# Flamingo block with a routed expert layer: the scores of a batch computed jointly, and the attention loop reordered on every engine

## The chip, the cores and the metric

The kernel runs on one core of a Trainium2 chip. The metric is the device time of one execution in microseconds (us), lower is better. A core has five engines with a queue of their own each: TensorE (PE in the profile; PEld are its weight loads), VectorE (DVE), ScalarE (ACT), GpSimd (POOL) and SyncE (SP), which issues DMAs. They run their queues in order and wait for one another through semaphores.

## The reference

```python
x = x + tanh(g_xattn) * xattn(layernorm(x), ctx)          # x: 16 x 128 x 128, ctx: 16 x 77 x 96
x = x + tanh(g_ffn) * experts(layernorm(x))

def xattn(x, y):                                          # 16 heads of 8
    q = x @ Wq.T + bq;  k, v = split(y @ Wkv.T + bkv)
    att = softmax(q @ k.T / sqrt(8))                      # per head, 128 x 77
    return (att @ v) @ Wo.T + bo

def experts(x):                                           # 4 rounds, 4 experts, top 2
    for r in range(4):
        w = softmax over the 2 largest of x @ Wg[r] + bg[r]
        x = x + sum_e w[e] * (gelu(x @ W1[e] + b1[e]) @ W2[e] + b2[e])
    return x
```

All is float32. Matmuls that need it are split in a high and a low part (float32r) and done as three passes: high by high, high by low, low by high.

## The kernel before

The 16 batches form four chunks of four. A prologue loads and transposes the weights and makes K, Q and V of chunk 0. Then comes the attention loop, one step per batch b = 0 to 15, and then the expert part, 64 units (round, chunk, expert) of 24 matmuls each, whose code the change leaves alone.

Step b of the loop works on several batches at once. TensorE computes the scores of batch b+1 (`scores`, line 1217), transposes the probabilities of batch b in three groups (`transpose_probs`, 1234; keys ("PT", b, 0..2)), multiplies those of batch b-1 with the values and, for the sums, with ones (`weigh_values`, 1246), and projects the output of batch b-2 (`project_o`, 1268). Scores of a batch lie in four PSUM banks, one per group of four heads (q = 0 to 3); each uses 32 rows of the array. They are made in two halves, q = 0, 1 and q = 2, 3: half 0 early in the step, half 1 after the products with the values. Half 0 is read by VectorE (`smallest`, 864: the minimum per head; `shift`, 874: subtracts it into `shifted`) and ScalarE takes one exponential of 616 columns from there. Half 1 is read by VectorE for the minimum and by ScalarE in eight exponentials of 77 columns straight from PSUM (`exponentials`, 665). The halves of the next batch may be written when those are done.

The rest of the probabilities' way: ScalarE copies each transposed group to SBUF (`move_pt`, 681), VectorE divides the product by the sums (`normalise_o`, 884: reciprocal and product) and adds the residual (`add_residual`, 893). In between, steps carry the work of the next chunk: by r = b % 4 the context is transposed and K made (r = 0), x transposed and Q made (r = 1), VectorE's low part of Q (`low_q`, 843; r = 2), V made (r = 3). Tables name the step for others: NORMALISE for VectorE's normalising of x of chunks 2 and 3, MOMENTS for the means and variances, SPLIT_X, ROUTER and WEIGHTS slots for the routing of the first two chunks. At b = 3 VectorE also splits the router weights (lines 1100 to 1111).

GpSimd multiplies K of batch b+2 with a head mask (`stage_k`, 551: a masked copy, a masked rounded copy, and their difference), adds the bias to x (`add_bias`, 567), and splits an eighth of the expert weights in each step of W_AT, one step later (W_LAG). It needs the weights that its own casting DMAs brought (lines 587 and 589).

Transposes and projections share two PSUM banks in turn (`next_job`): a job may be written when the last but one has been read. The order of all of it is written out by hand in one loop per engine; TensorE's is

```python
if b + 1 < B: scores(b + 1, 0)
transpose_probs(b, 0)
...
if b >= 1: weigh_values(b - 1)
if b + 1 < B: scores(b + 1, 1)
transpose_probs(b, 1)
transpose_probs(b, 2)
if b >= 2: project_o(b - 2)
```

with the chunk work between, and an extra pair of matmuls on the identity before group 2 (WARM_PT) whose result is not used. ScalarE's order is copy of group 0, long exponential of b+1, copies of groups 1 and 2, eight short exponentials of b+1.

## Time and profile before

| | us |
|---|---|
| median of the timed executions | 489.18 |
| all three | 489.18, 484.53, 489.44 |
| the profiled execution | 485.13 |
| its span, first to last instruction | 483.4 |
| granted TensorE clock, mean | 0.996 of full |

Rows of the profile give a start in us from the beginning of the span, a duration, the engine, the line of the kernel, the operation with output and inputs, and how many instructions are merged (xN). Durations overlap slightly where an engine is pipelined, so what one instruction costs is best read from start to start. What stands in brackets is how long the engine had been idle and who ended it.

### The profile page before, as it was taken

How to read it: one execution, taken by the hardware profiler on the slowest of the kernel's cores; microseconds unless marked ns; L12 is line 12 of the kernel's file. 1: busy time of each engine (PE TensorE's matmuls, PEld its weight loads, DVE VectorE, ACT ScalarE, POOL GpSimd, SP SyncE). 2: the span in 40 equal slices, each digit the busy share in tenths (PEclk: the TensorE clock that was granted, in tenths of full speed). 3: DMA queues.
4: the chain of work that ended last, by engine and by line, in shares of the span. 5: the costliest groups of instructions: out<-in, count | busy, mean ns of one | idle time of the engine just before them, and what ended most of it. 6: DMA issues, size and time to landing. Idle time of an engine off the chain costs nothing.

```text
span 483.4 us, 9118 instructions
## 1 busy us (share of the span) xinstructions
PE 471.8 (98%) x3007; PEld 383.4 (79%) x3007; DVE 374.6 (77%) x750; ACT 383.0 (79%) x783; POOL 82.8 (17%) x133
## 2 busy tenths in 40 slices
PE   7799999989999999999999999999999999999997
PEld 6578787878888788888888888888888888888885
DVE  4869888897888867876887687778777976886776
ACT  2588888769787887988788788869886988798773
POOL 6567597920500000000000000000000000000000
PEclk9899999999999999999999999999999999999999
DMA  5920000004002020030031004000400040014001
GB/s 146 296 75 15 3 15 3 14 1 177 2 0 89 1 89 0 22 155 1 1 120 57 1 0 177 0 1 1 176 0 0 4 174 1 1 43 155 23 1 44
DMA packets 15173, 25.21 MB, mean 52 GB/s; under 512 B 3505, under 2 KB 11542, under 8 KB 13078
## 3 DMA queue, kind: packets, MB, share of 16 engines
q1 hardware_dynamic: 11152, 22.05, 13.3%
q0 software_dynamic: 2592, 2.10, 2.1%
q10 hardware_dynamic: 1382, 0.49, 0.5%
q8 instruction: 24, 0.39, 0.3%
q14 instruction: 23, 0.19, 0.1%
HBM read 22.82 MB, written 1.18 MB: 50 GB/s over the span
## 4 chain that ended last, share of the span: by engine, by line
PE 92%; DVE 4%; issue 2%; ACT 1%; POOL 1%; ACTq 0%; POOLq 0%; DVEq 0%
PE ps L1361 12%; PE ps L1348 12%; PE ps L1363 12%; PE ps L1362 12%; PE ps L1350 12%; PE ps L1349 12%; PE ps L1243 5%; PE ps L1230 3%; PE ps L1259 3%; PE ps L1169 2%; PE ps L1264 2%; PE ps L1271 1%; DVE xn L840 1%; PE ps L1204 1%; PE ps L1314 1%
## 5 line engine op out<-in xcount | busy, mean ns | idle before, releaser
L922 DVE TENSOR_TENSOR h_lo<-g_sb,h_hi 128x512 fp32r<-128x512 f32 x256 | 169.9, 687 | 75.5 <-ACT h_hi L786 75.4
L779 ACT ACTIVATE g_sb<-ps,cols 128x512 f32<-128x512 f32 x256 | 174.7, 693 | 35.2 <-PE ps L1350 34.2
L786 ACT ACTIVATE h_hi<-g_sb 128x512 fp32r<-128x512 f32 x256 | 155.8, 640 | 0.0
L1361 PE MATMUL ps<-h_hi,w_hi 128*128 128x512 f32 x252 | 101.5, 403 | 0.0
L1348 PE MATMUL ps<-x_hi,w_hi 128*128 128x512 f32 x256 | 101.1, 395 | 0.0
L1350 PE MATMUL ps<-x_hi,w_lo 128*128 128x512 f32 x256 | 100.1, 391 | 0.0
L1349 PE MATMUL ps<-x_lo,w_hi 128*128 128x512 f32 x256 | 99.8, 390 | 0.0
L1363 PE MATMUL ps<-h_hi,w_lo 128*128 128x512 f32 x252 | 99.6, 395 | 0.0
L1362 PE MATMUL ps<-h_lo,w_hi 128*128 128x512 f32 x252 | 99.5, 395 | 0.0
L1350 PEld LDWEIGHTS ps<-x_hi,w_lo 128*128 128x128 f32 x256 | 48.0, 188 | 11.3
L1349 PEld LDWEIGHTS ps<-x_lo,w_hi 128*128 128x128 f32 x256 | 48.1, 188 | 10.9
L1348 PEld LDWEIGHTS ps<-x_hi,w_hi 128*128 128x128 f32 x256 | 48.0, 188 | 10.9 <-issue 0.2
L1363 PEld LDWEIGHTS ps<-h_hi,w_lo 128*128 128x128 f32 x252 | 47.2, 187 | 11.8
L1361 PEld LDWEIGHTS ps<-h_hi,w_hi 128*128 128x128 f32 x252 | 47.3, 188 | 11.0
L1362 PEld LDWEIGHTS ps<-h_lo,w_hi 128*128 128x128 f32 x252 | 47.3, 188 | 10.3
L943 DVE TENSOR_TENSOR cur<-cur,contrib 128x512 f32<-128x512 f32 x63 | 43.1, 684 | 0.0
L686 ACT ACTIVATE probT<-ps 103x512 f32<-103x512 f32 x48 | 29.3, 613 | 11.1 <-PE ps L1243 10.1
L871 DVE TENSOR_REDUCE least<-ps 128x8 f32<-128x616 f32 x32 | 25.4, 793 | 11.2 <-PE ps L1230 11.1
L1243 PE MATMUL ps<-ident,prob 128*103 128x128 f32 (+1 forms) x192 | 31.4, 286 | 0.0
L677 ACT ACTIVATE prob<-ps,least 128x77 f32<-128x77 f32 x128 | 29.2, 345 | 1.1 <-DVE least L871 1.1
L1243 PEld LDWEIGHTS ps<-ident,prob 128*103 128x103 f32 (+1 forms) x192 | 22.5, 162 | 5.7 <-issue 4.5
L932 DVE SCALAR_TENSOR_TENSOR contrib<-ps,cols,cwb_even 128x512 f32<-128x512 f32 x32 | 23.9, 746 | 1.1 <-PE ps L1363 1.0
(149 smaller groups left out, 492.6 us busy)
## 6 DMA issues: line engine op xcount, KB each, us to landing
cwb_even<-cw_rows SPq DMA_DIRECT2D x8, 1024.0 KB, 5.3
cwb_odd<-cw_rows SPq DMA_DIRECT2D x8, 1024.0 KB, 4.7
w_hi<-in_L_ffn_W_dram POOLq DMA_DIRECT2D x2, 1024.0 KB, 13.4
x_sb<-in_x_dram SPq DMA_DIRECT2D x4, 256.0 KB, 7.6
w_in<-in_L_ffn_W_dram SPq DMA_DIRECT2D x1, 1024.0 KB, 5.7
out_dram<-xn SPq DMA_DIRECT2D x3, 256.0 KB, 2.3
ctx_sb<-in_ctx_dram ACTq DMA_DIRECT2D x4, 115.5 KB
v_st<-v_sb SPq DMA_DIRECT2D x8, 38.5 KB
```

The lines of the kernel that those rows point to most:

```text
L686: nc.scalar.activation(probT[0:RP, b % 2, PG * g:PG * (g + 1), :], bank(("PT", b, g))[0:RP, :].rearrange("p (c l) -> p c l", l=L), ACT.Cop ...
L779: nc.scalar.activation(g_sb[:, k, :], ps[:, k, :], ACT.Gelu_apprx_tanh, bias=b1_c[:, e * NF + k:e * NF + k + 1]).then_inc(gelu_done, 1)
L786: nc.scalar.activation(h_hi[:, u % 2, k, :], g_sb[:, k, :], ACT.Copy).then_inc(hi_done, 1)
L922: nc.vector.tensor_tensor(h_lo[:, u % 2, k, :], g_sb[:, k, :], h_hi[:, u % 2, k, :].bitcast(F32), ALU.subtract).then_inc(lo_done, 1)
L943: nc.vector.tensor_tensor(cc, cc, contrib[:, u % 2, :], ALU.add).then_inc(added, 1)
L1243: t = tr(bank(key)[0:n, k * L:(k + 1) * L], prob[:, b % 2, at:at + n], ident[:, :])
L1348: mm(ps[:, k, :], w1_hi[:, w], x_hi[:, c, :], start=True, stop=False)
L1349: mm(ps[:, k, :], w1_hi[:, w], x_lo[:, c, :], start=False, stop=False)
L1350: mm(ps[:, k, :], w1_lo[:, w], x_hi[:, c, :], start=False, stop=True).then_inc(w1_done, 1)
L1361: mm(yb, w2_hi[:, w], hh, start=k == 0, stop=False)
L1362: mm(yb, w2_hi[:, w], hl, start=False, stop=False)
L1363: m = mm(yb, w2_lo[:, w], hh, start=False, stop=k == NF - 1)
```

## The change

The scores of a batch are made in one set: each of the three passes runs over all four groups q, and the set waits for the subtraction and for all short exponentials of the batch before. All loops are reordered: TensorE does scores, groups 2 and 1, projection of b-2, chunk work, group 0, values of b-1; ScalarE copies groups 2 and 1, does the short exponentials, copies group 0, does the long one; VectorE starts a step with the division and the minimum of half 1. VectorE, not ScalarE, copies group 2 of step 0 and group 0 of step 11 (PT_DVE). K is split in high and low once per chunk (`split_k`, for chunk 0 `split_k0` on VectorE), so that staging it takes two masked copies and no difference. The bias is added to four batches in one instruction. The warm pair in the loop is gone; some of the prologue's are moved, and the prologue is reordered. The two casting DMAs of the expert weights are issued by GpSimd in steps 1 and 0 of the loop. MOMENTS, NORMALISE, SPLIT_X, W_AT and other slots shift by a step in places; low_q runs in r = 1. In both kernels x of chunks 2 and 3 is normalised on VectorE (NORMALISE_P, the table for GpSimd, is empty).

```diff
-        XT_AT = (10, 12)
+        XT_AT = (10, 14)
-        GATE0_SLOT = 13
+        GATE0_SLOT = 14
-        WEIGHTS0_SLOT = 15
+        WEIGHTS0_SLOT = 14
-        WARM_PT = (0, 0, 1)
-        R_LOW = 2
+        R_LOW = 1
+        R_LK = 2
+        PT_DVE = {0: 2, 11: 0}
+        FIRST_E = 1
+        WD_AT = (1, 0)
...
-        NORMALISE = {4: 2, 8: 3}
-        MOMENTS = {1: (0, 2), 5: (0, 3), 7: (1, 0), 10: (1, 1), 14: (1, 2)}
-        SPLIT_X = {11: 0, 13: 1}
+        NORMALISE = {3: 2, 8: 3}
+        NORMALISE_P = {}
+        MOMENTS = {0: (0, 2), 3: (0, 3), 7: (1, 0), 10: (1, 1), 15: (1, 2)}
+        SPLIT_X = {11: 0, 14: 1}
...
-        W_AT = (2, 3, 5, 6, 8, 10, 11, 13)
+        W_AT = (3, 4, 6, 7, 8, 9, 10, 13)
...
+            def split_k(c):
+
+                at = slice(TC * M * c, TC * M * (c + 1))
+                moved(pool, ("K", c))
+                pool.wait_ge(k_split, 2 * c)
+                nc.gpsimd.tensor_copy(kT_r[:, :], kT[:, at]).then_inc(k_split, 1)
+                pool.wait_ge(k_split, 2 * c + 1)
+                nc.gpsimd.tensor_tensor(kT_lo[:, at], kT[:, at], kT_r[:, :].bitcast(F32),
+                                        ALU.subtract).then_inc(k_split, 1)
...
-                nc.gpsimd.tensor_tensor(k_f[:, :, :], kb, headm, ALU.mult).then_inc(k_stage, 1)
-                nc.gpsimd.tensor_tensor(k_hi[:, s, :].rearrange("p (h m) -> p h m", m=M), kb, headm,
+                nc.gpsimd.tensor_tensor(k_hi[:, s, :].rearrange("p (h m) -> p h m", m=M),
+                                        kT[:, at].unsqueeze(1).to_broadcast([P, HQ, M]), headm,
                                         ALU.mult).then_inc(k_stage, 1)
-                pool.wait_ge(k_stage, 3 * b + 2)
-                nc.gpsimd.tensor_tensor(k_lo[:, s, :], k_f[:, :, :].rearrange("p h m -> p (h m)"), k_hi[:, s, :].bitcast(F32),
-                                        ALU.subtract).then_inc(k_stage, 1)
+                nc.gpsimd.tensor_tensor(k_lo[:, s, :].rearrange("p (h m) -> p h m", m=M),
+                                        kT_lo[:, at].unsqueeze(1).to_broadcast([P, HQ, M]), headm,
+                                        ALU.mult).then_inc(k_stage, 1)
...
-            def scores(b, half):
+            def scores(b):
 
                 c, at = b // TC, slice(b % TC * L, b % TC * L + L)
-                if half == 0:
-                    moved(pe, ("Q", part_of(b)))
-                    pe.wait_ge(k_stage, 3 * b + 3)
-                if b >= 1 and half == 0:
+                moved(pe, ("Q", part_of(b)))
+                pe.wait_ge(k_stage, 2 * b + 2)
+                if b >= 1:
                     pe.wait_ge(sub_done, b)
-                if b >= 1 and half == 1:
-                    pe.wait_ge(exp_done, 2 * b)
+                    pe.wait_ge(exp_done[1], b)
                 for n, (qs, ks) in enumerate(passes):
-                    for q in (2 * half, 2 * half + 1):
+                    for q in range(NQ):
```

TensorE, in a step with r = 3 of before, from the first half of the scores to the second; L1230 are scores, L1243 transposes of probabilities, L1259 and L1264 the products with values and ones.

```order
L1230 MATMUL ps<-k_hi,q_hi 128x308 x2
L1230 MATMUL ps<-k_lo,q_hi 128x308 x2
L1230 MATMUL ps<-k_hi,q_lo 128x308 x2
L1243 MATMUL ps<-ident,prob 103x128 x2
L1243 MATMUL ps<-ident,prob 102x128
L1243 MATMUL ps<-ident,prob 103x128
L1259 MATMUL ps<-probT,v_st 32x128 x12
L1264 MATMUL ps<-probT,row_head 32x128 x12
L1230 MATMUL ps<-k_hi,q_hi 128x308 x2
L1230 MATMUL ps<-k_lo,q_hi 128x308 x2
L1230 MATMUL ps<-k_hi,q_lo 128x308 x2
```

The same engine and kind of step in the kernel after; L1285 are scores, L1300 the transposes, L1330 the projection (the products with the values follow later, after group 0).

```order
L1285 MATMUL ps<-k_hi,q_hi 128x308 x4
L1285 MATMUL ps<-k_lo,q_hi 128x308 x4
L1285 MATMUL ps<-k_hi,q_lo 128x308 x4
L1300 MATMUL ps<-ident,prob 102x128
L1300 MATMUL ps<-ident,prob 103x128 x2
L1300 MATMUL ps<-ident,prob 102x128
L1300 MATMUL ps<-ident,prob 103x128
L1300 MATMUL ps<-ident,prob 102x128
L1300 MATMUL ps<-ident,prob 103x128 x2
L1330 MATMUL ps<-wT,oT_sb 128x128
```

The six pairs of scores have become three groups of four at the head of the step, and the products with the values have moved from its middle to its end.

VectorE in step 3 of before, from the minimum of half 1 to the start of step 4's normalising; L1102 to L1110 are the split of the router weights, L897 the residual, L871 the minima, L880 the subtraction, L887 and L891 the division, L840 the normalising of chunk 2.

```order
L871 TENSOR_REDUCE least<-ps 128x8
L1102 CAST wg_s<-wg_in 128x4x4
L1104 TENSOR_TENSOR wg_s<-wg_in,wg_s 128x4x4
L1108 CAST wg_w<-wg_in 128x16x4
L1110 TENSOR_TENSOR wg_w<-wg_in,wg_w 128x16x4
L897 SCALAR_TENSOR_TENSOR x_sb<-ps,tgates,x_sb 128x128
L871 TENSOR_REDUCE least<-ps 128x8
L880 TENSOR_TENSOR shifted<-ps,least 128x616
L887 RECIPROCAL rT_sb<-ps 128x128
L891 TENSOR_TENSOR oT_sb<-ps,rT_sb 128x128
L840 TENSOR_SCALAR xn<-x_sb,mv,rstd 128x128 x4
```

VectorE in step 3 of after, from the minimum of half 1 to the end of the step; L1141 to L1149 are the split, L882 the normalising of chunk 2, L873 and L876 the moments of chunk 3.

```order
L917 TENSOR_REDUCE least<-ps 128x8
L951 SCALAR_TENSOR_TENSOR x_sb<-ps,tgates,x_sb 128x128
L1141 CAST wg_s<-wg_in 128x4x4
L1143 TENSOR_TENSOR wg_s<-wg_in,wg_s 128x4x4
L1147 CAST wg_w<-wg_in 128x16x4
L1149 TENSOR_TENSOR wg_w<-wg_in,wg_w 128x16x4
L917 TENSOR_REDUCE least<-ps 128x8
L926 TENSOR_TENSOR shifted<-ps,least 128x616
L882 TENSOR_SCALAR xn<-x_sb,mv,rstd 128x128 x4
L873 BN_STATS stats<-x_sb 128x6 x4
L876 BN_AGGR mv<-stats 128x2 x4
```

The split now stands ahead of the second minimum and the subtraction, and the normalising and the moments have moved into the same step.

ScalarE in step 0 of before: L686 copies, L671 long and L677 short exponentials, L626 context, L643 K.

```order
L686 ACTIVATE probT<-ps 103x512
L626 ACTIVATE ctxT<-ps 96x308
L671 ACTIVATE prob<-shifted 128x616
L686 ACTIVATE probT<-ps 103x512 x2
L643 ACTIVATE kT<-ps,cols 128x308
L677 ACTIVATE prob<-ps,least 128x77 x8
```

ScalarE in step 0 of after, with the end of the prologue ahead of it: L693 x and L701 Q of batches 1 to 3, L716 short and L710 long exponentials, L785 the wide bias, L665 context, L725 copies, L682 K.

```order
L716 ACTIVATE prob<-ps,least 128x77 x8
L693 ACTIVATE xnT<-ps 128x384
L701 ACTIVATE q_hi<-ps,bq_s 128x384
L710 ACTIVATE prob<-shifted 128x616
L785 ACTIVATE bv_w<-ident,cols 128x128
L665 ACTIVATE ctxT<-ps 96x308
L725 ACTIVATE probT<-ps 103x512
L716 ACTIVATE prob<-ps,least 128x77 x8
L682 ACTIVATE kT<-ps,cols 128x308
L725 ACTIVATE probT<-ps 103x512
L710 ACTIVATE prob<-shifted 128x616
```

The short exponentials of batch 0 stand ahead of x and Q of batches 1 to 3, and in the loop the short ones come before the long one.

## Rows read from the trace of the kernel before

**Rows 1.** Stretches of the core: each engine's busy us, clock, DMA share, GB/s.

```profile
19.52:108.77 89.25, 87.36 (x1239) 71.21 (x1238) 74.59 (x172) 72.48 (x209) 64.14 (x97) 0.99 0.11 33
200.00:300.00 100.00, 100.00 (x437) 80.90 (x436) 77.39 (x143) 82.88 (x154) 0.00 (x0) 1.00 0.14 57
```

The columns of rows 1 are the stretch, its length, then PE, PEld, DVE, ACT and POOL busy with their instructions, the granted clock of PE, the DMA share and GB/s.

**Rows 2.** Timeline of PE, step 6 to 7: start us, us, engine, line.

```profile
55.96 0.41 PE L1230 MATMUL ps<-k_hi,q_hi 32*128 32x308 f32 x2
...
56.57 0.68 PE L1243 MATMUL ps<-ident,prob 128*103 128x128 f32 x4
57.09 0.39 PE L1169 MATMUL ps<-ident 128*128 128x128 f32 x2
57.31 0.60 PE L1243 MATMUL ps<-ident,prob 128*102 128x128 f32 x4
...
59.30 0.89 PE L1259 MATMUL ps<-probT,v_st 103*32 103x128 f32 x24
...
60.78 0.41 PE L1230 MATMUL ps<-k_hi,q_hi 32*128 32x308 f32 x2
```

**Rows 3.** Timeline of PE, the first scores of the kernel.

```profile
13.20 0.43 PE L1230 MATMUL ps<-k_hi,q_hi 32*128 32x308 f32 x4
...
13.58 0.34 PE L1230 MATMUL ps<-k_hi,q_lo 32*128 32x308 f32 x4
```

**Rows 4.** Timeline of ACT, steps 0 and 1.

```profile
25.09 1.83 ACT L677 ACTIVATE prob<-ps,least 128x77 f32<-128x77 f32 x8
26.75 0.66 ACT L686 ACTIVATE probT<-ps 103x512 f32<-103x512 f32 x1
27.23 0.67 ACT L654 ACTIVATE xnT<-ps 128x512 f32<-128x512 f32 x1
27.71 0.80 ACT L671 ACTIVATE prob<-shifted 128x616 f32<-128x616 f32 x1
```

**Rows 5.** Groups of DVE, 26.92 to 106.5: count, busy us, mean ns, idle before.

```profile
L871 DVE TENSOR_REDUCE least<-ps 128x8 f32<-128x616 f32 x27 | 21.4, 794 | 9.2 <-PE ps L1230 9.1
L887 DVE RECIPROCAL rT_sb<-ps 128x128 f32<-128x128 f32 x14 | 13.3, 947 | 0.0
L880 DVE TENSOR_TENSOR shifted<-ps,least 128x616 f32<-128x616 f32 x14 | 11.2, 798 | 0.4
L897 DVE SCALAR_TENSOR_TENSOR x_sb<-ps,tgates,x_sb 128x128 f32<-128x128 f32 x13 | 4.4, 336 | 1.7 <-PE ps L1271 1.4
...
L891 DVE TENSOR_TENSOR oT_sb<-ps,rT_sb 128x128 f32<-128x128 f32 x14 | 4.1, 292 | 0.5
```

**Rows 6.** Timeline of DVE, chunk work at five places.

```profile
13.06 2.31 DVE L840 TENSOR_SCALAR xn<-x_sb,mv,rstd 128x128 f32<-128x128 f32 x3
...
39.78 0.16 DVE L1102 CAST wg_s<-wg_in 128x16 fp32r<-128x16 f32 x1
...
40.69 0.82 DVE L1110 TENSOR_TENSOR wg_w<-wg_in,wg_w 128x64 fp32r<-128x64 f32 x1
...
44.82 1.90 DVE L840 TENSOR_SCALAR xn<-x_sb,mv,rstd 128x128 f32<-128x128 f32 x4
...
67.26 1.16 DVE L840 TENSOR_SCALAR xn<-x_sb,mv,rstd 128x128 f32<-128x128 f32 x4
...
103.86 0.86 DVE L831 BATCH_NORM_STATS2 stats<-x_sb 128x6 f32<-128x128 f32 x4
```

**Rows 7.** Timeline, three marks: second scores, last exponentials, first expert matmul.

```profile
19.52 0.62 PE L1230 MATMUL ps<-k_hi,q_hi 32*128 32x308 f32 x2
...
104.67 1.83 ACT L677 ACTIVATE prob<-ps,least 128x77 f32<-128x77 f32 x8
...
108.77 0.47 PE L1348 MATMUL ps<-x_hi,w_hi 128*128 128x512 f32 x1
```

**Rows 8.** DMA issues: count, KB each, median us from issue to landing.

```profile
w_hi<-in_L_ffn_W_dram POOLq DMA_DIRECT2D x2, 1024.0 KB, 13.4
```

**Rows 9.** Groups of POOL, 26.92 to 106.5: the masked copies of K.

```profile
L561 POOL TENSOR_TENSOR k_hi<-kT,head_mask 128x308 fp32r<-128x308 f32 x12 | 8.5, 706 | 0.0
```

More of the change, by code:

```diff
@@ L368, in bank, with probs_read @@
             return ps[:, jobs[key][2], :]
+        def probs_read(b):
+            return max(jobs[("PT", b, g)][0] for g in range(3)) + 1
         LN = [(0, "a"), (0, "b"), (0, 1), (0, 2), (0, 3), (1, 0), (1, 1), (1, 2), (1, 3)]
@@ L665, in exponentials @@
             def exponentials(b, half):
[L667 to L668 removed]
+                if b >= 2 and half == FIRST_E:
+                    act.wait_ge(job_mm, probs_read(b - 2))
                 if half == 0:
@@ L1111, in _ @@
                                             ALU.subtract).then_inc(wg_split, 1)
+                if b + 1 < B:
+                    smallest(b + 1, 0)
+                if b == WEIGHTS0_SLOT:
+                    weights(0)
+                if b + 1 < B:
+                    shift(b + 1)
+                if b == ROUTER0_SLOT:
+                    router(0)
+                if b in SPLIT_X:
+                    split_x(SPLIT_X[b])
+                if b in NORMALISE:
+                    normalise(NORMALISE[b])
+                if b in MOMENTS:
+                    moments(*MOMENTS[b])
+                if b == ROUTER1_SLOT:
+                    router(1)
+                if c < NC and r == R_LOW:
+                    low_q(c)
             normalise_o(B - 2)
+            weights(1)
             add_residual(B - 3)
-            weights(1)
             normalise_o(B - 1)
@@ L1248, in weigh_values @@
                 c = b // TC
-                moved(pe, ("PT", b, 2))
+                pe.wait_ge(job_act, max(read_no[("PT", b, g)] for g in range(3) if PT_DVE.get(b) != g))
+                if b in PT_DVE:
+                    moved(pe, ("PT", b, PT_DVE[b]))
                 pe.wait_ge(v_ld[c], 16 * len(pieces))
```

314 lines of the change are left out of this document (164 added, 150 removed).

## The prediction, made before the changed kernel was run

> **What bounds the kernel now.** I read the busy table in stretches first, because the kernel has two halves with different limits. From 200 to 300 us (the mixture of experts) TensorE is busy 100.00 of 100 us and VectorE and ScalarE 77.39 and 82.88 [rows 1]; that code is the same in both kernels, so it can only start earlier or later. The attention loop, 19.52 to 108.77 us, shows TensorE 87.36, VectorE 74.59, ScalarE 72.48, GpSimd 64.14 of 89.25 us [rows 1]. Over its 16 steps (b = 0 to 15, the last one partly) TensorE is the bound, but by little: divided by 15 steps, VectorE has 4.97 us of work per step and ScalarE 4.83 us, against 5.95 us that pass. So no more than about 1 us a step can be won, whatever TensorE is relieved of.
>
> Second, the order of time on TensorE in one step without chunk work, 55.96 to 60.78 us [rows 2]: half of the scores 0.61 (55.96 to 56.57), a transpose group 0.52, two warm instructions 0.22, and so on without a hole, the other half of the scores among it, the two products with the values 1.48 (59.30 to 60.78): 4.82 us, all TensorE.
>
> Third, the first scores of the kernel, the only place where both halves stand back to back with nothing between them [rows 3]: the twelve matmuls (three groups of four) start at 13.20 and the last ends at 13.58 + 0.34 = 13.92, 0.72 us. Half of them alone takes 0.61 to the next instruction. Four row groups of the array thus run side by side, and a joint set costs what half a set costs.
>
> **The change, part by part.** TensorE: each step loses one half of scores, 0.61, and the warm pair, 0.22, from rows 2: 0.83 us. A plain step falls from 4.82 to 3.99, one with chunk work by as much. Over 14 steps that is 11.6 us of TensorE, if TensorE still set the pace. It does not.
>
> ScalarE after: per step the eight short exponentials 1.83 busy (25.09), a copy every 0.48 when they stand in a row (26.75, 27.23, 27.71), the long exponential 0.80 [rows 4]: 1.8 + 3 x 0.48 + 0.8 = 4.0 us, and some 0.8 of chunk work on average (4.83 in all, above). The order changes: eight short ones first, the long one last.
>
> VectorE after: two minima at 0.79, the subtraction 0.80, reciprocal 0.95, product 0.29, residual 0.34 [rows 5]: 3.96 us, 3.8 with the overlap of neighbours. The joint scores couple them more tightly: the scores of batch b+1 need the subtraction of b AND all exponentials of the short half of b, and both minima now wait for one signal. In a plain step: scores 0.7, minimum 0.8, residual 0.3, minimum 0.8, subtraction 0.8 gives 3.4 us from one set of scores to the next, below ScalarE's 4.0 to 4.5; this chain alone costs nothing. What costs is chunk work in front of it. Two probability copies move to VectorE (steps 0 and 11, 0.65 us each by the nearest row, 0.79 for a 616-wide read, at most; at least 0.48, ScalarE's).
>
> Step 3 is the crowded one. VectorE now has the split of the router weights (39.78 to 40.69 + 0.82, so 1.73), the normalising of chunk 2 (1.90 for four in step 4 of before) and the moments of chunk 3 (0.86 for the four statistics and 0.4 behind them) [rows 6] in one step; before they stood in steps 3, 4 and 5. With its 3.8 of its own this makes 8.3 us, and a product that TensorE waits for (the output projection) stands behind it.
>
> I laid the three queues side by side with these prices, those of the chunk work from rows 6 and the like, the orders of before and after, and the waits of the code. From the end of the last exponential of step 0 to that of step 14, the steps 1 to 14 come out as 5.2, 4.55, 5.3, 6.9, 5.45, 4.55, 4.45, 5.25, 5.8, 4.55, 5.85, 4.95, 4.0, 5.95: 72.75 us. Steps near 4.5 are ScalarE's plus a wait for the first minimum; 5.2 to 5.8 are those where K and the context, or x and Q of the next chunk, pass through ScalarE and TensorE in turn; 6.9 is step 4, which pays step 3's backlog; 5.85 and 5.95 are VectorE's (split of x, router and weights). Before, the same stretch runs from 25.09 + 1.83 = 26.92 [rows 4] to 104.67 + 1.83 = 106.50 [rows 7], 79.58 us. Won: 6.8 us.
>
> Prologue: K is split on VectorE before it is staged, so the first scores come 0.6 late; the eight short exponentials of batch 0 (1.83) now stand before x of batches 1 to 3 is moved for Q; and the bias product waits behind the long one. The second scores start at some 22.3 instead of 19.52 [rows 7]. As all exponentials of batch 0 are done by then, step 0 is shorter, and its end moves only from 26.92 to 27.95: lost 1.0 us.
>
> Tail: before, the first matmul of the experts comes 108.77 - 106.50 = 2.27 us after the last exponential [rows 7]. After, more stands between them: the transposes that need the long exponential, the weights' transpose, the output projection, which waits 1 us for VectorE (behind the split of x), router logits 1.1, a transpose group 0.55 and the value products 1.48 [rows 2]: 5.2 us. Lost: 2.9 us.
>
> Sum: -6.8 + 1.0 + 2.9 = -2.9; I add 0.05 us per step for hand-overs that the layout took at nothing (14 x 0.05): -2.2 us. GpSimd loses one of three products per batch and gains two short splits per chunk, and stays a step ahead; its cast loads of the expert weights move from the start into steps 0 and 1. They took 13.4 us from issue to landing [rows 8]; issued at about 27 and 30 they are there by 44, and the first split of weights in step 4 stands near 43: a wait of about 1 us, covered, since the K that GpSimd stages behind it is wanted near 48.7.
>
> The profiled execution took 485.13 us with a span of 483.4, so the sum gives 482.9. The three timed executions of before are 489.18, 484.53 and 489.44: two levels 4.5 us apart, whatever the kernel does. Against the median the same sum gives 487.0. I name the middle, 485.0 us, and let the range hold both.
>
> **Rivals.** Packed: the backlog of step 3 is absorbed and steps fall to the 4.97 us that VectorE needs (14 x 4.97 = 69.6): another 3.1 us less, 479.8 against the profile, 483.8 against the median. For it: VectorE's idle time before the minima in the loop, 9.2 us [rows 5], was a wait for scores that now come at once. Against it: VectorE's chunk work is lumped, and the loop that joins the scores leaves no half to work on meanwhile. To reach it the gain must be 5.3 us, just over 1% (4.9 us, about what a measurement of this kernel can tell from no change).
>
> VectorE slowed by GpSimd: three normalisings took 2.31 beside GpSimd's products (13.06), 0.77 each, against 1.90 and 1.16 for four at 44.82 and 67.26 [rows 6]; and a subtraction of 64 elements per partition took 0.82 where a cast of 16 took 0.16 [rows 6]. If both normalisings of the loop meet GpSimd like that, each costs 4 x 0.77 = 3.1 instead of the 1.5 that I took (between the two), and as VectorE sets steps 4 and 9 both times show: +3.2, so 1.0 us slower than before, 486.1 against the profile, 490.2 against the median. It decides from 2.6 us each on. For it: GpSimd is busy 72% of the loop [rows 1]. Against it: one product of 0.71 less on GpSimd per batch [rows 9]. The Trainium skill (SBUF — State Buffer, Who interferes with whom) states that a tensor_scalar in a two-port mode and a GpSimd instruction exclude each other for a whole instruction, the later one blocking fully. By that rule, as an estimate, each of four would wait for a GpSimd product, 4 x (0.29 + 0.71) = 4.0 [rows 6, 9], two times 2.5 more than I took, and the sum would be 2.8 us slower than before; the row of 2.31 fits it, the row of 1.90 shows half of it.
>
> Weights late: the cast loads, issued in the loop, are squeezed behind the plain loads of the same weights and the values' small transfers and land after 45.8, from when K of batch 6 is late. At twice 13.4 us behind the second issue, 57, the loss is 11 us: slower by 9, 494. Against it: the transfers of that stretch are few (the x, context and projection loads are over by then), so landing should be quicker, not slower.
>
> **How the numbers follow.** Forecast (within 1%) 0.55, packed 0.2, slowed VectorE 0.17, weights late 0.08. Faster by over 1%: the packed case and a little of the forecast's own spread, 0.28. Slower by over 1%: late weights and the bad end of the slowed case, 0.11. Within 1%: 0.61. The range runs from 479.5 (packed, lower level) to 489.6 (slowed, upper level).
>
> **What would show it.** Right: joint scores as three groups of four in 0.72 us or less; loop steps of 4.5 without and 5.2 to 5.8 with chunk work, the step after the router-weight split near 7; TensorE with real holes in the loop, waiting for exponentials and minima; second scores near 22, last exponential near 101.4, first expert matmul 106 to 107; the expert half unchanged at some 375 us (483.4 - 108.77). Wrong: if joint scores take 1.2 us, the array did not run four groups; if step 4 is 5.3, the packed case holds; if GpSimd waits at its first weight split for more than 3 us, the loads were late; if the expert half differs by over 1 us, the clock or the router's tail has moved.

## The result and the profile after

| | before | after |
|---|---|---|
| median, us | 485.08 (484.42 to 489.44, 20 executions) | 488.62 (485.45 to 491.81, 20 executions) |
| ratio after / before | | 1.0055, interval 1.0033 to 1.0077 |
| profiled execution, us | 485.13 | 485.45 |
| its span, granted clock | 483.4, 0.996 | 483.7, 0.993 |

The change makes the kernel 0.55% slower; the forecast was a small gain (482.9 against the profile, 485.0 named). By the ratio that is 2.7 us (the medians lie 3.5 apart). Between the two profiled executions the difference is only 0.3 us; the rest is not in these two traces at all, and that is the lesson of this case. In what follows a hole is a stretch in which TensorE stands idle between two matmuls; half clock is the lower level of its granted clock; warm pairs are matmuls on the identity whose result is not used.

The busy table in stretches, kernel after. The columns are those of [rows 1]: stretch, length, then PE, PEld, DVE, ACT, POOL busy, PE's clock, DMA share, GB/s.

```profile
26.00:27.00 1.00, 0.92 (x2) 0.75 (x3) 0.96 (x3) 1.00 (x7) 0.96 (x3) 0.52 0.44 119
27.00:31.00 4.00, 4.00 (x25) 3.13 (x24) 3.24 (x12) 2.56 (x6) 3.83 (x6) 0.50 2.02 291
...
32.00:34.00 2.00, 2.00 (x8) 1.10 (x6) 0.00 (x0) 1.74 (x7) 0.00 (x0) 0.78 0.97 275
34.00:104.70 70.70, 65.30 (x1079) 52.06 (x1078) 62.72 (x135) 60.30 (x176) 44.04 (x61) 1.00 0.04 10
...
200.00:300.00 100.00, 100.00 (x437) 81.00 (x436) 77.45 (x144) 82.77 (x155) 0.00 (x0) 1.00 0.15 59
```

The expert half is what it was. In the loop TensorE is no longer the bound: busy 65.30 of 70.70 us, VectorE 62.72, ScalarE 60.30. The column to look at is PE's clock. From about 26 to 32.8 us it is half of full (0.50 is the lower of the two levels, 1.2 GHz against 2.4). In the trace of before there is such a stretch too, of half the length and earlier:

```profile
17.20:20.60 3.40, 3.40 (x17) 2.57 (x15) 3.09 (x13) 2.73 (x11) 1.88 (x3) 0.50 2.05 253
21.00:25.00 4.00, 3.58 (x31) 2.64 (x29) 2.23 (x4) 3.09 (x7) 3.81 (x7) 1.00 1.02 370
```

What TensorE did before the clock fell, kernel after: its timeline in step 0.

```profile
21.86 0.31 PE L1285 MATMUL ps<-k_hi,q_lo 32*128 32x308 f32 x4
22.11 0.47 PE L1235 MATMUL ps<-ident,ctx_sb 77*96 77x77 f32 x4
22.42 1.36 PE L1300 MATMUL ps<-ident,prob 128*102 128x128 f32 x8
26.08 1.39 PE L1243 MATMUL ps<-ctxT,wT 96*128 96x308 f32 x2 [2.30 <-DVE probT L935]
27.27 1.06 PE L1300 MATMUL ps<-ident,prob 128*103 128x128 f32 x4
```

It stands still from 23.78 to 26.08, and the next matmuls take 1.39 and 1.06 us, where at full clock the same two groups take 0.79 and 0.68 (in the run with the normalising moved, below). The releaser in brackets is VectorE's copy of a transposed group. VectorE at the same time:

```profile
21.86 2.86 DVE L882 TENSOR_SCALAR xn<-x_sb,mv,rstd 128x128 f32<-128x128 f32 x4
24.64 0.79 DVE L917 TENSOR_REDUCE least<-ps 128x8 f32<-128x616 f32 x1
25.35 0.67 DVE L935 COPY probT<-ps 103x512 f32<-103x512 f32 x1
```

and GpSimd beside it:

```profile
22.03 1.29 POOL L603 TENSOR_TENSOR x_sb<-x_sb,bo_row 128x512 f32<-128x512 f32 x1 [1.01 <-DVE bo_row L1125]
23.29 0.69 POOL L591 TENSOR_TENSOR k_hi<-kT,head_mask 128x308 fp32r<-128x308 f32 x1
23.95 0.69 POOL L594 TENSOR_TENSOR k_lo<-kT_lo,head_mask 128x308 fp32r<-128x308 f32 x1
```

Four normalisings of chunk 1 take 2.86 us, where the best four of before took 1.16 [rows 6]. They stand ahead of a minimum and a copy that everything waits for, and they meet GpSimd's products, the first of which is the new bias addition for four batches at once. Read one by one, the four take 0.34, 1.30, 0.73 and 0.74 us: the last three are about as long as the three products beside them (1.29, 0.69, 0.69), and each ends 0.08 or 0.09 us after one of them. In the kernel before, the same four stood ahead of `bo_row`, the bias row that GpSimd's addition waits for:

```profile
19.59 1.17 DVE L840 TENSOR_SCALAR xn<-x_sb,mv,rstd 128x128 f32<-128x128 f32 x4 [0.27 <-POOL rstd L539]
```

They were over at 20.76, and GpSimd's addition began at 21.11. In the kernel after they stand behind `bo_row`, which ends at 21.94 and so releases GpSimd's addition (22.03) just as they begin.

The rest of the profile after answers to the prediction's list. The first scores, and the wait of step 4:

```profile
14.08 0.41 PE L1285 MATMUL ps<-k_hi,q_hi 32*128 32x308 f32 x4 [0.97 <-DVE k_lo L907]
...
14.44 0.34 PE L1285 MATMUL ps<-k_hi,q_lo 32*128 32x308 f32 x4
...
46.27 0.41 PE L1285 MATMUL ps<-k_hi,q_hi 32*128 32x308 f32 x4 [1.33 <-DVE shifted L926]
```

A joint set takes 14.44 + 0.34 - 14.08 = 0.70 us, as [rows 3] said, and the first one starts 0.88 us later than in before. VectorE in step 3, the router split that stands ahead of the second minimum (L917) and of the subtraction that row 46.27 waits for:

```profile
41.88 0.49 DVE L1141 CAST wg_s<-wg_in 128x16 fp32r<-128x16 f32 x1
42.40 0.62 DVE L1143 TENSOR_TENSOR wg_s<-wg_in,wg_s 128x16 fp32r<-128x16 f32 x1
42.95 0.79 DVE L1147 CAST wg_w<-wg_in 128x64 fp32r<-128x64 f32 x1
43.77 0.70 DVE L1149 TENSOR_TENSOR wg_w<-wg_in,wg_w 128x64 fp32r<-128x64 f32 x1
44.39 0.79 DVE L917 TENSOR_REDUCE least<-ps 128x8 f32<-128x616 f32 x1
45.22 0.80 DVE L926 TENSOR_TENSOR shifted<-ps,least 128x616 f32<-128x616 f32 x1
45.93 1.11 DVE L882 TENSOR_SCALAR xn<-x_sb,mv,rstd 128x128 f32<-128x128 f32 x4
```

VectorE's groups in the loop (29.57 to 104.66), answering to [rows 5]:

```profile
L917 DVE TENSOR_REDUCE least<-ps 128x8 f32<-128x616 f32 x28 | 22.0, 790 | 0.7 <-PE ps L1285 0.7
L941 DVE RECIPROCAL rT_sb<-ps 128x128 f32<-128x128 f32 x14 | 13.3, 949 | 1.7 <-PE ps L1323 1.7
```

The idle time ahead of the minima has gone from 9.2 to 0.7 us: VectorE no longer waits for scores, scores wait for it. From the end of one step's last exponential to the next's, steps 1 to 14 take 6.69, 4.61, 5.90, 6.77, 5.44, 4.61, 4.26, 5.91, 5.56, 5.33, 4.71, 5.23, 4.27, 5.80: 75.09 us, from 29.57 to 104.66 (before 79.58). The tail: last exponential of step 14, then the first matmul of the experts.

```profile
103.87 0.79 ACT L710 ACTIVATE prob<-shifted 128x616 f32<-128x616 f32 x1
...
109.09 0.50 PE L1407 MATMUL ps<-x_hi,w_hi 128*128 128x512 f32 x1
```

And the weights' cast loads, in the DMA issues:

```profile
w_hi<-in_L_ffn_W_dram POOLq DMA_DIRECT2D x2, 1024.0 KB, 8.1
```

### The profile page after: what moved, and what is told of

It reads as the page before. It is cut to its first block, busy times and chain, and to the rows that moved or that the text cites. A ratio compares the mean times of both kernels' runs of the same rounds, so it can differ in the third digit from the quotient of the medians.

```text
span 483.7 us, 9099 instructions
## 1 busy us (share of the span) xinstructions
PE 464.2 (96%) x2989; PEld 375.8 (78%) x2989; DVE 376.2 (78%) x753; ACT 381.0 (79%) x781; POOL 72.3 (15%) x112
## 4 chain that ended last, share of the span: by engine, by line
PE 85%; DVE 7%; issue 3%; ACT 2%; DMA 1%; SPq 1%; DVEq 0%; ACTq 0%
PE ps L1420 12%; PE ps L1407 12%; PE ps L1422 12%; PE ps L1421 12%; PE ps L1409 12%; PE ps L1408 12%; PE ps L1300 3%; PE ps L1318 2%; PE ps L1323 2%; DMA gates<-in_g_ffn_dram 1%; PE ps L1285 1%; DVE least L917 1%; DVE rT_sb L941 1%; PE ps L1261 1%; DVE xn L882 1%
## 5 line engine op out<-in xcount | busy, mean ns | idle before, releaser
L725 ACT ACTIVATE probT<-ps 103x512 f32<-103x512 f32 x46 | 27.4, 616 | 9.4 <-PE ps L1300 9.2
L716 ACT ACTIVATE prob<-ps,least 128x77 f32<-128x77 f32 x128 | 29.3, 349 | 5.1 <-DVE least L917 5.0
L1300 PE MATMUL ps<-ident,prob 128*103 128x128 f32 (+1 forms) x192 | 30.5, 294 | 1.0 <-issue 0.4
L1300 PEld LDWEIGHTS ps<-ident,prob 128*103 128x103 f32 (+1 forms) x192 | 23.4, 169 | 7.0 <-ACT probT L725 2.8
L917 DVE TENSOR_REDUCE least<-ps 128x8 f32<-128x616 f32 x32 | 25.0, 789 | 0.7 <-PE ps L1285 0.7
L741 ACT ACTIVATE th<-half_d 128x32 f32<-128x32 f32 (+1 forms) x10 | 2.2, 225 | 28.7 <-DVE half_d L1046 28.7
```

Source lines behind the costliest of these rows:

```text
L917: nc.vector.tensor_reduce(least[:, b % 2, :].rearrange("p (q h) -> p q h", q=NQ)[:, two, :], scores, AX.X, ALU.min).then_inc(least_done[ha ...
L1300: t = tr(bank(key)[0:n, k * L:(k + 1) * L], prob[:, b % 2, at:at + n], ident[:, :])
```

## The granted clock separates the executions of one kernel

Every timed execution comes with its span and mean granted clock. Sorted by clock, before is a ladder: of 35 executions beside the first experiments 13 have 0.996 and 484.25 to 484.97 us, 4 have 0.993 and 485.8 to 486.1, 12 have 0.991 and 486.2 to 486.5, 6 have 0.985 or 0.986 and 489.1 to 489.4. After has one at 0.993 (485.45, the one that was profiled), four at 0.989 or 0.984 (486.5 to 487.8), ten at 0.985 or 0.986 (488.2 to 489.5), five at 0.981 or 0.978 (490.3 to 491.8). Time at half clock is 2 x (1 - clock) x span; the mean is 7.6 us for before and 15.0 us for after. A line through each kernel's executions costs 0.44 us (before) and 0.40 us (after) per us of half clock, and reaches full clock at 482.8 and 482.9. Put in the two means, the lines give 0.40 x 15.0 - 0.44 x 7.6 + 0.1 = 2.8 us, which is 488.93 - 486.15. That the two agree is no test, since a fitted line always goes through its means; what the lines say is that the kernels' times lie close to one common line and differ in where on it they are.

One limit holds for all comparisons with after below: after was timed in one series of 20 executions, and no run repeats it beside the variants. The ratios, each against before of the same series, are the safer measure.

So two theories went to the chip. A: the change made holes in TensorE's work, the one of 2.3 us in step 0 first, after which the clock is halved, and more so in most executions than in the profiled one. B: the pairs of warm matmuls that the change removed from the loop had kept the clock up.

## Experiments

All are edits of the kernel after unless it is said. Each ratio is against before on the same chip.

**1. The copy of step 0 back to ScalarE.**

```diff
-        PT_DVE = {0: 2, 11: 0}
+        PT_DVE = {11: 0}
```

> Edit: in the changed kernel the copy of probability group 2 of step 0 goes back from VectorE to ScalarE; nothing else. In the profile of the changed kernel TensorE stands idle for 2.3 us (23.8 to 26.1) until VectorE has made that copy, behind 2.86 us of normalising, and its granted clock falls to half at 26 for 6.8 us. Theory A (the median is slow because that hole lowers the clock): the hole shrinks to some 0.7 us, the last exponential of step 0 comes 1 us or more earlier, the mean granted clock of the executions rises from 0.986 towards 0.993, and the median falls by 2 to 4 us, to 485 to 487. Theory B (the clock is a bystander and the time lies in the lengthened prologue and tail): the median falls by the 1 us of step 0 at most, clock as it is.

Measured: 486.92 us (485.98 to 488.54), ratio 1.0022 (1.0000 to 1.0043), 10.3 us at half clock. The copy was not what mattered: the hole moved behind it, as long as before.

```profile
25.43 0.68 PE L1300 MATMUL ps<-ident,prob 128*103 128x128 f32 x4
28.40 0.46 PE L1285 MATMUL ps<-k_hi,q_hi 32*128 32x308 f32 x4 [2.29 <-POOL k_lo L594]
```

The bracket names GpSimd's k_lo, but K of this batch was staged by 25.6 (that of the next one ended at 28.37, by chance just before; in run 5 the same scores start ahead of it). What the scores wait for stands on VectorE and ScalarE of this run, in order of time:

```profile
22.82 2.87 DVE L882 TENSOR_SCALAR xn<-x_sb,mv,rstd 128x128 f32<-128x128 f32 x4
25.61 1.49 DVE L917 TENSOR_REDUCE least<-ps 128x8 f32<-128x616 f32 x2
...
26.43 1.83 ACT L716 ACTIVATE prob<-ps,least 128x77 f32<-128x77 f32 x8 [1.05 <-DVE least L917]
```

Normalising, minimum, short exponentials (to 28.26), scores at 28.40. The cause of the hole is the normalising, whoever copies. The last exponential of step 0 is not earlier (29.76), and yet there is less half clock than the 15.0 us of after. This run serves below as a control: it keeps a hole of 2.29 us.

**2. The hole of step 0 filled with ten warm pairs.**

```diff
                 transpose_probs(b, 1)
+                if b == 0:
+                    moved(pe, ("V", 0))
+                    warm(ps[:, 7, 0:P], 10)
```

> Edit: in the changed kernel ten warm matmuls on the identity (20 instructions, some 2.2 us at full clock) stand in that hole of step 0, written to a free bank; TensorE would wait there anyway, so no wait is taken away. Theory A: the granted clock stays up in the loop, step 1 falls from 6.7 to about 5.3 us, mean clock 0.99 or more, median 2 to 4 us lower. Theory B: no change of the median beyond 0.5 us, even where the clock is higher.

Measured: 485.99 (483.95 to 486.77), ratio 0.9985 (0.9960 to 1.0010), 5.0 us at half clock. No dependency is shorter, TensorE does more, and the kernel is 2.6 us faster than after; the intervals of the two ratios do not touch. Against run 1, which keeps the hole and was timed in the same series, the means are 485.65 and 487.24, and the half clock 5.0 against 10.3 us. Its trace:

```profile
23.55 2.40 PE L1226 MATMUL ps<-ident 128*128 128x128 f32 x20
26.02 0.79 PE L1243 MATMUL ps<-ctxT,wT 96*128 96x308 f32 x2
26.65 0.60 PE L1300 MATMUL ps<-ident,prob 128*103 128x128 f32 x4
```

The same matmuls at 26 us take 0.79 and 0.60 instead of 1.39 and 1.06, step 0 takes 8.06 us instead of 8.84 (from one last exponential to the next; it ends at 28.73 instead of 29.57) and step 1 takes 5.68 instead of 6.69: 1.79 us in all, which is what the half clock cost the profiled execution of after. Two executions of this run were at full clock all through: 483.95 and 483.98 us. The clock falls here at another place, the tail:

```profile
103.00:115.00 12.00, 11.75 (x130) 9.44 (x130) 6.15 (x27) 7.26 (x14) 4.40 (x6) 0.72 0.24 89
```

**3. The router weights split two steps later.**

```diff
-                if b == 3:
+                if b == 5:
                     dve.wait_ge(moe_ld...
```

> Edit: in the changed kernel the split of the router weights moves from step 3 to step 5 of VectorE; the rest is as it was. Step 4 of the changed kernel took 6.8 us, as forecast, and step 3 5.9, because VectorE has the split, the normalising of chunk 2 and the moments of chunk 3 in one step. If that backlog is what steps 3 and 4 pay, they fall by some 2 us together and step 5 (where VectorE idles 1.7 us) grows by under 1: the median 1 to 1.5 us lower. If the steps are bound otherwise, no change.

Measured: 483.85 (482.07 to 487.05), ratio 0.9951 (0.9924 to 0.9979). Steps 3 and 4 take 4.24 and 6.38 (from 5.90 and 6.77), step 5 5.44 as before: 2.05 us. So step 3 was the crowded one, as the prediction had it. The split itself costs less in step 5. The median fell by more than the 1 to 1.5 us expected, since half clock (8.1 us) is rarer as well; up to the edit at 42 us this run is the kernel after, with its hole of 2.30 us in step 0, so the edit can't be why there is less of it before that point. The half clock of step 0 begins here only after 28 us, and step 0 takes 8.07 us, not 8.84.

**4. The kernel before without its warm pairs in the loop.**

```diff
-        WARM_PT = (0, 0, 1)
+        WARM_PT = (0, 0, 0)
```

> Edit: the kernel before without its warm pair in the loop (0.22 us per step on TensorE). If TensorE's queue sets the pace of the loop of before, 14 to 15 steps lose 0.2 us each: 3 us faster, 482. If the pair earned its place by the clock, the mean granted clock falls below 0.99 and the time is no lower or higher than before. If the steps are bound by ScalarE and VectorE just behind TensorE, under 1 us.

Measured: 484.79 (483.92 to 488.64), ratio 0.9973 (0.9951 to 0.9996), 7.2 us at half clock. The first expert matmul comes 1.0 us earlier, not the 14 x 0.22 = 3.1 that a loop bound by TensorE alone would give: a plain step gains 0.15 to 0.17, one with chunk work mostly 0.06 or less. Theory B, as a statement on before, falls: the loop of before keeps its clock without the pairs (1.00 from 21 to 108 us in this trace).

**5. Chunk 1 normalised at the end of step 0 instead of ahead of its first minimum.**

```diff
-        NORMALISE = {3: 2, 8: 3}
+        NORMALISE = {0: 1, 3: 2, 8: 3}
...
-            normalise(1)
```

> Edit: in the changed kernel VectorE normalises x of chunk 1 at the end of step 0 (behind the subtraction) instead of ahead of the loop. There it took 2.86 us beside GpSimd's products (four tensor_scalars, 1.17 in the kernel before), and both the first minimum of batch 1 and the copy that TensorE waits for stood behind it. Theory A (that contended normalising makes the hole that lowers the clock): the 2.3 us hole of TensorE at 24 us is gone, the last exponential of step 0 comes 2 us earlier (27.5 instead of 29.57), the mean time at half clock falls from 15 us per execution to 10 or less, median 3 to 4 us lower (485). Theory B (the clock falls for other reasons, such as the missing warm pairs): the hole goes and 1 to 2 us with it, time at half clock stays at 15 us.

Measured: 482.38 (481.56 to 484.42), ratio 0.9931 (0.9903 to 0.9959), 1.7 us at half clock: 6.2 us less than after, the largest effect of one edit in this study. VectorE, then TensorE of this run:

```profile
21.94 0.80 DVE L917 TENSOR_REDUCE least<-ps 128x8 f32<-128x616 f32 x1 [0.35 <-PE ps L1284]
22.70 0.69 DVE L935 COPY probT<-ps 103x512 f32<-103x512 f32 x1
...
24.85 2.61 DVE L882 TENSOR_SCALAR xn<-x_sb,mv,rstd 128x128 f32<-128x128 f32 x4
```

```profile
22.07 1.36 PE L1299 MATMUL ps<-ident,prob 128*102 128x128 f32 x8
23.45 0.79 PE L1242 MATMUL ps<-ctxT,wT 96*128 96x308 f32 x2
24.11 0.68 PE L1299 MATMUL ps<-ident,prob 128*103 128x128 f32 x4
25.92 0.42 PE L1284 MATMUL ps<-k_hi,q_hi 32*128 32x308 f32 x4 [1.13 <-ACT prob L716]
```

The normalising costs nearly as much (2.61), but nobody waits for it. The hole is 1.1 instead of 2.3 us, step 0 ends at 27.27, and the mean clock of the execution is 1.000. Step 0 takes 6.90 us against the 8.06 of run 2, at full clock there as well: 1.16 us are the wait. The remaining 0.30 us between the two ends (27.27 and 28.73) had arisen ahead of the edit: run 9, with the same code up to step 3, starts step 0 0.86 us later than run 5. What is left of the 6.2 us goes with the clock, as far as the runs show. A hole of 1.1 us is no guarantee of full clock, though: run 10 has the same one, and the clock of its profiled execution falls at 28 us.

**6. One warm pair ahead of group 1 in steps 1 to 15.**

```diff
                 claim(key)
+                if g == 1 and b >= 1:
+                    warm(bank(key)[:, 0:P], 1)
```

> Edit: one warm pair per step (0.22 us) comes back into the loop of the changed kernel, from step 1 on, ahead of transpose group 1, where TensorE waits for the long exponential anyway. Theory B (the missing pairs let the clock fall): time at half clock falls from 15 us to 10 or less, median 2 us or more lower. Theory A (it falls at the hole of step 0, which holds no pair in either kernel, and in the tail): time at half clock and median within 1 us of the changed kernel's.

Measured: 485.76 (484.56 to 486.65), ratio 0.9992 (0.9964 to 1.0020), 5.2 us at half clock: 2.9 us less than after. Steps 2 to 6 keep their lengths to 0.02 us (the pair stands in waits), steps 7 and 8 grow by 0.2 each, step 1 is still at half clock (6.62). None of its 12 executions is under a clock of 0.991, where 16 of after's 20 are at 0.986 or below. Runs 1, 3 and 7, which keep the hole of step 0 too, had 10.3, 8.1 and 9.8 us at half clock; run 7 is of the same series as this one. So in the kernel after, whose loop has waits, pairs seem worth something, and B is partly right for it, by fewer us than the comparison with after's 15.0 suggests.

**7. Chunks 2 and 3 normalised on GpSimd.**

```diff
-        NORMALISE = {3: 2, 8: 3}
-        NORMALISE_P = {}
+        NORMALISE = {}
+        NORMALISE_P = {3: 2, 8: 3}
```

> Edit: in the changed kernel x of chunks 2 and 3 is normalised on GpSimd (steps 3 and 8) instead of VectorE. VectorE's backlog of step 3 loses 1.1 us, so step 4 falls from 6.77 to some 5.7; GpSimd, idle for 4 us in step 4, takes 3.3 us for four of them at its rate in the kernel before. Step 8 (5.91) falls by under 0.5. Median 1 to 1.5 us lower; no change if GpSimd's K of batch 6 is late by it; time at half clock as in the changed kernel (15 us).

Measured: 485.56 (482.62 to 487.44), ratio 0.9997 (0.9971 to 1.0023), 9.8 us at half clock. On GpSimd four take

```profile
39.37 3.13 POOL L580 TENSOR_SCALAR xn<-x_sb,mv,rstd 128x128 f32<-128x128 f32 x4
```

and VectorE is relieved in steps 3 and 4 (5.18 and 5.75 instead of 5.90 and 6.77); step 8 stays 5.91. That is 1.74 us off two steps: of the two places for this work VectorE is the dearer one here, and GpSimd has slack in the loop. The kernel after is 3 us slower than this in the median; the rest goes with the half clock, 9.8 us where 15 were expected. Up to step 3 this run is the kernel after as well, and there it fares no better: steps 1 and 2 take 7.36 and 4.81, at half clock.

**8. The kernel before with six warm matmul pairs behind its first scores.**

```diff
             scores(0, 1)
+            warm(bank("BO")[:, 0:P], 6)
             transpose_xn("b")
```

> Edit: the kernel before with six warm matmuls (12 instructions) behind the first scores, where TensorE idles 1.6 us and then again until 16.7, and behind which its clock falls at 17.2 us. If the granted clock is what separates executions of one kernel (484.5 at 0.996, 486.4 at 0.991, 489.2 at 0.986 in the executions of before), time at half clock falls from 7.6 us per execution to 5 or less, and the median by 1 to 2 us, with no instruction of the computation moved. If the clock is a bystander, no change.

Measured: 484.82 (484.39 to 485.58), ratio 0.9977 (0.9953 to 1.0000), 0.3 us at half clock; 17 to 21 us are at full clock in its trace. The upper rungs of the ladder (486.4, 489.2) are gone, but the lowest is where it was (484.39, before 484.42): the half-clock stretch at 17.2 us, the only one in the profile of before, costs nothing, since TensorE waits for others there. So the line of before must not be read down to full clock; the ten executions of this run at full clock lie at 484.4 to 485.1, 484.7 on the mean. The line of after must not be read down either. No execution of after ran at full clock, but its profiled one without the 1.79 us of run 2 would have taken 483.7, and the two executions of run 2 at full clock, whose dependencies are after's, took 484.0: an estimate of 483.7 to 484.0 for after at full clock, 0.7 to 1.0 below before.

**9 and 10. Edits 5 and 3 together (9), and then also x of batches 1 to 3 moved ahead of the exponentials of batch 0 (10).**

```diff
-            exponentials(0, 1)
             move_xn("b")
+            exponentials(0, 1)
```

> Edit: in the changed kernel both earlier single edits together: chunk 1 normalised at the end of step 0, and the router-weight split in step 5 instead of step 3. If the two act on different stretches and add, steps 3 and 4 fall from 5.54 and 6.76 to some 4.2 and 6.4 us (1.7 to 2 us off the 482.4 of the first alone), so 480.5, with time at half clock of 3 us or less per execution. If one gain hid behind the other, or a clock interval comes back because all later work shifts, 481.5 or more.

> Edit: the same two edits, and ScalarE moves x of batches 1 to 3 ahead of the eight short exponentials of batch 0, as the kernel before did. My forecast charged the prologue's new order with 1.0 us at the end of step 0, most of it this. If it is right, the second scores come 1 us or more earlier (at 20 instead of 21.1) and the median is 0.5 to 1.2 us below the two edits'. If VectorE (low part of Q, bias row) or the exponentials then hold step 0, no change.

Measured: 481.24 (480.77 to 483.82), ratio 0.9900 (0.9865 to 0.9935), and 479.91 (479.30 to 485.46), ratio 0.9889 (0.9834 to 0.9944). In the steps the two edits add as expected: steps 3 and 4 take 4.26 and 6.25, 1.79 us less than in run 5. The median gains 1.1 on run 5, since there is more half clock (4.6 against 1.7 us). Run 10's median is 1.3 below run 9's, of the few executions that there are. Its own profiled execution can't show whether the second scores come earlier, being at half clock there; run 12, with the same order at full clock, can: 6.64 us from the first scores to the second, 7.40 in run 9. In run 10 four executions at a clock of 1.0 took 479.3 to 480.0, one at 0.993 483.6 and the profiled one at 0.985 485.46: the same code, 6 us apart. Its windows show where:

```profile
12.00:17.00 5.00, 3.66 (x28) 3.18 (x29) 4.12 (x10) 1.19 (x3) 1.36 (x2) 0.78 0.18 32
...
28.00:34.00 6.00, 6.00 (x69) 4.49 (x64) 4.56 (x13) 5.05 (x15) 4.29 (x7) 0.72 1.78 317
34.00:102.00 68.00, 64.42 (x1053) 51.29 (x1043) 62.13 (x135) 59.49 (x173) 44.12 (x61) 1.00 0.05 13
102.00:112.00 10.00, 9.76 (x79) 7.77 (x78) 5.78 (x27) 4.76 (x10) 4.46 (x6) 0.66 0.30 107
```

Three stretches, around 15, 30 and 107 us. The profile of run 1 has all three as well, that of run 3 the first two, that of run 7 the last two, those of after and of run 6 only the one around 30, those of runs 2 and 11 only the last; those of runs 5 and 9 have none. Up to 15 us the code of all of these is the same, so the first stretch comes and goes with no edit behind it.

**11. As 9, and the moments of chunk 3 two steps later.**

```diff
-        MOMENTS = {0: (0, 2), 3: (0, 3), 7: (1, 0), 10: (1, 1), 15: (1, 2)}
+        MOMENTS = {0: (0, 2), 5: (0, 3), 7: (1, 0), 10: (1, 1), 15: (1, 2)}
```

> Edit: the same two edits, and the moments of chunk 3 go from step 3 back to step 5, where they stood before. Theory: step 4 is long because VectorE's queue of step 3 is (moments 1.2 us of it). Then step 4 falls from 6.4 to some 5.3, step 5 grows by under 0.3, and the median is 1 us below the two edits'. If step 4 is held by something else (K and the context on ScalarE), it stays at 6.4 and so does the time.

Measured: 483.16 (481.73 to 484.03), ratio 0.9931 (0.9901 to 0.9961), not the gain that was expected. Step 4 falls by 0.34 to 5.91, steps 5 and 6 grow by 0.14 and 0.47: the work was not taken from the path, it was moved along it. The rest of the 1.9 us over run 9 goes with 6.4 us at half clock against 4.6; the profiled execution has it in the tail (clock 0.76 from 100 to 107 us, the first expert matmul 5.7 us after the last exponential instead of 4.4). Why there is more half clock here, the traces do not show.

**12. As 10, with warm pairs ahead of group 1 in the last four steps (two in step 15).**

> Edit: the three edits of the run with x moved first, and warm pairs in the waits of the last four steps (one in steps 12 to 14, two in step 15, ahead of transpose group 1, where TensorE waits for the long exponential 0.4 us in step 15). Theory: of the half-clock time left (3.5 us per execution on the mean), the part that costs stands at 102 to 112 us, where TensorE waits and does logits of 8 columns. If the pairs hold the clock there, executions at 0.985 to 0.993 (483.6 and 485.5) disappear and all lie within 479.3 to 480.5. If the tail's clock falls for the logits themselves, the spread stays and the median rises by up to 0.5 us.

Measured: 479.66 (479.15 to 481.75), ratio 0.9869 (0.9813 to 0.9924), 1.4 us at half clock. It beats both kernels: 1.3% under before. Against run 10 the median is the same and the slow executions are missing (six of each, so this is weak). Its tail, at full clock, takes 103.16 - 98.74 = 4.42 us from last exponential to first expert matmul, as after's does:

```profile
99.00:104.00 5.00, 4.73 (x71) 4.02 (x71) 4.65 (x23) 1.84 (x6) 2.47 (x4) 1.00 0.20 82
104.00:477.00 373.00, 369.94 (x1683) 300.03 (x1681) 287.39 (x546) 303.07 (x556) 8.69 (x9) 1.00 0.13 48
```

## Why the prediction was wrong, step by step

Right, with small errors:

- Joint scores: 0.70 us measured, 0.72 forecast. Four row groups run side by side. The first ones came 0.88 late, forecast 0.6.
- The loop. The bound moves off TensorE and the saving of 11.6 us on it mostly does not show. Steps 2 to 14 sum to 68.40 us; the forecast was 67.55 and 13 x 0.05. Step 4 was forecast at 6.9 and took 6.77, the wait of 1.33 us for the subtraction being step 3's backlog; run 3 confirmed it by undoing it. The router split took 2.51 us (41.88 to 44.39), not 1.73, the normalising 1.11, not 1.5: two errors that partly cancel. (The 8.3 us of step 3 in the prediction is a sum with 1.5 for the normalising, not with the 1.90 that it names.) Steps 10 and 11 came out 0.78 longer and 1.14 shorter than laid out, steps 3 and 8 0.6 longer.
- The tail: 4.43 us, forecast 5.2.
- Weights late: dead. They landed in 8.1 us, and GpSimd came to its first weight split (40.27) without a wait.
- Packed: dead. Steps 1 to 14 sum to 75.09 us, not 69.6, and step 4 paid for step 3.
- The expert half: 483.7 - 109.09 = 374.6 us, unchanged.

Wrong, against the profiled execution (482.9 forecast, 485.45 measured):

- "Step 0 is shorter, and its end moves only from 26.92 to 27.95: lost 1.0 us." It moved to 29.57. The second scores were early (21.48, forecast 22.3); the error lies behind them. I priced the copy on VectorE but not chunk 1's normalising ahead of it, although it stands in that queue: 2.86 us. Run 5, with it out of the way, does step 0 in 6.90 us; run 2, with it in place at full clock, in 8.06; after took 8.84, and the last 0.78 is the clock.
- Step 1: 5.2 forecast, 6.69 measured, of it 1.01 the clock (run 2: 5.68).
- Together 1.65 too little for step 0, 1.6 for the loop (nearly all of it step 1), 0.75 too much for the tail: the 2.5 us. Of these 1.79 are half clock.

Wrong, against the median, and this is the failed step: the sum has no term for TensorE's clock. I took the two levels of the timings of before, 484.5 and 489.4, as occurring "whatever the kernel does" and put the forecast in the middle. They are not: they are time at half clock (0.996 against 0.985), and how much of that a kernel gets depends in part on its holes. Runs 2 and 8 fill a hole and change nothing else, run 5 halves one, and time at half clock falls to 5.0, 0.3 and 1.7 us; run 6 (5.2) and run 12 (1.4, six executions) point the same way. The change gave TensorE 8 us less to do up to the first expert matmul (79.5 us busy from the second scores on, half clock included, against 87.4 in [rows 1]), left this time as waits, and half clock rose from 7.6 to 15.0 us per execution. Without it I had the sign but not the size: after's estimated 483.7 to 484.0 at full clock lies 0.7 to 1.0 us under before's 484.7, where the forecast had 2.2. Measured were 2.7 us in the other direction. The range was added up wrongly at its end, too: the slowed case at the upper level is named as 490.2, and the range stops at 489.6.

The rival "VectorE slowed by GpSimd" had the mechanism but not the place. I priced it for the normalisings of chunks 2 and 3, where VectorE sets the pace; these took 1.11 in step 3, while GpSimd stood idle (44.39 to 47.13), and 1.16 in step 8. It struck in step 0, by 2.86 - 1.16 = 1.7 us. That rival named a price of 3.1 us for four that meet GpSimd; 2.86, 2.87, 2.61, 2.61 and 2.58 were measured in step 0 of after and of runs 1, 5, 10 and 12. The Trainium skill (SBUF — State Buffer, Who interferes with whom) says that such an instruction and a GpSimd one exclude each other entirely. The estimate by that rule was 4.0 us for four; the rows show less than that, and more than the 1.9 that I had from [rows 6]. That a tensor_scalar waits out a product, the three of 1.30, 0.73 and 0.74 us bear out; that the product waits as well, they don't, since it took its usual 0.69. Nor did the row of 2.31 fit the rule, as I had written: by it three would have taken 3.0. In the prediction's words it "decides from 2.6 us each on": so it did, once.

What stays open: why after itself had 15.0 us at half clock, where runs 1, 3 and 7, which keep the hole of step 0 and up to step 3 differ from it by a copy at most, had 8.1 to 10.3. Chance from series to series is one answer, the tail another; the runs don't decide, and the effect of a single edit read against after's 488.62 is uncertain by some 2 us (an estimate, 5 us of half clock at 0.4). The change also moved warm pairs within the prologue and added some (29 where there were 22), and no run puts the old ones back. Open too: which wait of the tail lowers the clock near 107 us (the pairs of runs 6 and 12 reduce it without showing which); why executions of the same code differ in whether a hole is followed by half clock; and in how many executions of after each of the three stretches occurs, since only the mean clock is known of those that were not profiled. That they are the same three as in runs 1, 2, 3, 7, 10 and 11 is inferred.

## What to carry to other kernels

Look at the granted clock of every timed execution, not only the profiled one, before pricing a change: if the times form a ladder along it, a change of TensorE's holes can move executions from one level to another. Keep a variant that leaves the hole in beside those that fill it, in the same series. When work is taken off TensorE and another engine becomes the bound, list the holes that this opens and what fills them. Here the variant with 2.3 us of waiting halved in one place took 6.2 us less than after and 3.2 to 4.5 less than runs 1, 6 and 7, which kept it; filling the hole with unused matmuls brought 2.6 against after and 0.9 against run 1. And put an instruction whose duration depends on GpSimd behind what others wait for: run 5 did not make it shorter, only harmless.

## What the runs showed of the hardware that I had not expected

- One kernel's executions lie on separate levels of mean clock, 0.996, 0.993, 0.991, 0.985, with 484.5, 485.9, 486.4 and 489.2 us, and hardly anything between (in the later series of before also 0.983 with 490.8). Over its executions 1 us at half clock goes with about 0.4 us of time; the one stretch of step 0 in after cost 1.79 us for 6.8, less than that.
- Half clock where TensorE waits anyway can be free: 19 executions of before with it at 17.2 us (by their clock of 0.995 or 0.996) took 484.7 us on the mean, the ten of run 8 at full clock 484.7.
- Four identical tensor_scalars on VectorE took 1.11, 2.61 and 2.86 us in the same kernel but for one edit. Being busy is not what makes GpSimd a bad neighbour: beside its own normalising, in step 8 of after, four took

```profile
71.24 3.18 POOL L560 TENSOR_SCALAR xn<-x_sb,mv,rstd 128x128 f32<-128x128 f32 x4
...
71.44 1.16 DVE L882 TENSOR_SCALAR xn<-x_sb,mv,rstd 128x128 f32<-128x128 f32 x4
```

- The router split took 2.51 us beside GpSimd's weight splits and products of K, against 1.04 in step 5 of run 9 (49.99 to 51.03), where GpSimd made products of K for most of the time (49.32 to 50.71); its smallest cast (16 elements per partition) took 0.49 and 0.17. What makes this difference the runs do not show.
- A releaser in brackets can be a coincidence: in run 1 it named a product of GpSimd that had nothing to do with the wait, because it ended 0.03 us before.
